# Newton step and scale factor of a group norm moved from VectorE to GpSimd in a convolution kernel

## The chip, the cores and the metric

The kernel runs on one core of a Trainium2 chip. The metric is the device time of one launch, in microseconds (us). The engines are called by the profile's names: PE is TensorE (matrix products), DVE is VectorE, ACT is ScalarE, POOL is GpSimd, SP is SyncE, which here only issues transfers.

## What is computed

Input x holds 32 images of 128 channels with 56 rows of 56 columns, float32. Each image is normalised in 32 groups of 4 channels, convolved with 3x3 weights that are first made ternary, and added to x.

```python
def _gn(v, G=32, eps=1e-05):
    B_, C_, H_, W_ = v.shape
    g = v.reshape(B_, G, C_ // G, H_, W_)
    m = jnp.mean(g, axis=(2, 3, 4), keepdims=True)
    s = jnp.var(g, axis=(2, 3, 4), keepdims=True)
    return ((g - m) / jnp.sqrt(s + eps)).reshape(v.shape)
...
wq = _quantize(weight, Wp, Wn)
out = jax.lax.conv_general_dilated(x, wq, window_strides=(1, 1), padding=((1, 1), (1, 1)), ...)
return out + bias[None, :, None, None]
...
x = x + _L0_conv_ref(_gn(x), L0_conv_weight, L0_conv_bias, L0_conv_Wp, L0_conv_Wn)
```

## The kernel before, in words

The 128 channels lie on the 128 partitions; one image is 128 x 3136 float32. The program handles one image in a slot, and the engines work on neighbouring images at once: in the slot of image `now` PE multiplies `now`, while DVE and ACT prepare image `nxt`, and ACT takes the sums of image `far`. Each engine's order inside a slot is written out by hand in a function `emit`; engines wait for each other by semaphores alone. The loop body holds four slots, since x and y have four buffers each.

For the rows of the convolution, even and odd image rows are combined into four planes C, D, A, B of 128 x 1568 float32 (sums and differences of rows): `make_c` (L561), `make_d` (L567) and `make_a` (L573) on DVE, `difference_b` (L326) on POOL. Each plane is multiplied by the image's scale factor `norm_scale` (one number for each partition) and split in two float16 parts: HI on ACT (`make_hi`, L388) and LO, the scaled plane minus HI, on DVE (`make_lo`, L607). PE multiplies the parts by the weights, 24 matmuls for each plane (L766). ACT copies the products of C and D out of the accumulators (L373, L379), and DVE adds the products of A and B to them in four instructions (`output_rows`, L622). POOL then issues two transfers that add x to y (L339), and SP stores y.

The scale factor of `nxt` is made in a chain of small steps on 128 x 1 numbers. PE sums the squares (L757), DVE makes the negative variance (`variance`, L585), ACT takes the root (`root`, L440), DVE takes the reciprocal (`first_rstd`, L591), and DVE refines it by one Newton step in two instructions (`newton_factor`, L596, and `scale_of_x`, L602). ACT's `make_hi(nxt, C)` is the first instruction that reads the result, and it waits for the semaphore `scale_of_x_ready`. DVE reads it first in `make_lo(nxt, C)`, behind that HI.

In a slot of the loop DVE's order is: LO of D, variance of `nxt`, LO of A, planes C and D of `nxt`, the three small steps, LO of B, plane A of `nxt`, LO of C of `nxt`, four output instructions. "LO of D, A, B" are those of `now`. POOL's order is plane B of `nxt`, then the two transfers of `now`. Plane B waits for LO of B and LO of C on DVE (`lo_ready`), and it thus stands beside DVE's output instructions. There are 30 slots of this kind; the first two slots have orders of their own.

Of the kernel before, what the change touches and what calls it, by code (L numbers as in the profile page):

```python
# [6 lines left out]
P = 128  # L7
# [4 lines left out]
X_BUFS = 4  # L12
# [10 lines left out]
ALU = mybir.AluOpType  # L23
# [7 lines left out]
def conv_preact_kernel(nc, x, weight, bias, wp, wn, out):  # L31
# [15 lines left out]
    with ExitStack() as ctx:  # L47
        def sb(name, shape, dt=F32):
            return ctx.enter_context(nc.sbuf_tensor(name, shape, dt))

        def sem(name):
            return ctx.enter_context(nc.semaphore(name))
# [33 lines left out]
        neg_var = sb("neg_var", [P, X_BUFS])  # L86
        std = sb("std", [P, X_BUFS])
        rstd0 = sb("rstd0", [P, X_BUFS])
        newton = sb("newton", [P, X_BUFS])
        norm_scale = sb("norm_scale", [P, X_BUFS])  # L90


# [39 lines left out]
        var_ready = sem("var_ready")  # L132
        std_ready = sem("std_ready")
        rstd_ready = sem("rstd_ready")
        newton_ready = sem("newton_ready")
        scale_of_x_ready = sem("scale_of_x_ready")
        edges_ready = sem("edges_ready")
        plane_ready = [sem(f"plane_ready{j}") for j in range(4)]
# [61 lines left out]
        def b_slice(img):  # L200
            return slice(img.buf, img.buf + 1)
# [98 lines left out]
        def _(pool):  # L300
# [17 lines left out]
                                        pattern=[[-1, P]], channel_multiplier=1).then_inc(consts_ready, 1)  # L318

            def run(p):  # L320
                def difference_b(img):
                    pool.wait_ge(x_loaded[img.buf], img.turn * 32 + 32)
                    wait(pool, lo_ready[B], img.count())
                    pool.wait_ge(lo_ready[C], img.count(plus=1))
                    even = x_sb[img.buf][:, 0:H:2, :]
                    nc.gpsimd.tensor_tensor(plane[B][:, 0:PAIRS - 1, :], even[:, 0:PAIRS - 1, :], even[:, 1:, :],  # L326
                                            ALU.subtract).then_inc(plane_ready[B], 1)

                def add_residual(img, h):

                    written = img.half(h, 1, 1)
                    if not isinstance(written, int):
                        written = pool.to_reg(written)
                    pool.wait_ge(consts_ready, 2 + len(TURNS))
                    pool.wait_ge(even_done, written)
                    pool.wait_ge(odd_done, written)
                    y = y_sb[img.buf][:, 2 * ROWS * h:2 * ROWS * (h + 1), :].rearrange("p h w -> p (h w)")
                    of = (out_dram if p else x_dram)[img.count(plus=-p * N_IMG)][:, h * 2 * COLS:(h + 1) * 2 * COLS]
                    pool.dma_start(y, of, accum_op=ALU.add).then_inc(residual_added[img.buf][h], 16)  # L339

                def emit(prev, now, nxt, far):
                    if now and nxt:
                        difference_b(nxt)
                    if now and nxt:
                        add_residual(now, 0)
                        add_residual(now, 1)

                slots(p, pool, emit)

            run(0)  # L350
            pool.wait_ge(flag_ready, 1)
            with pool.If(pool.value_load(differ[0:1, 0:1], min_val=0, max_val=1) != 0):
# [142 lines left out]

        @block.vector
        def _(dve):
            nc.vector.memset(no_bias[:], 0.0).then_inc(zero_ready, 1)

            steps = [0]  # L500
# [44 lines left out]
            def run(p):  # L545
# [44 lines left out]
                    dve.wait_ge(std_ready, img.count(plus=1))  # L590
                    nc.vector.reciprocal(rstd0[:, b], std[:, b]).then_inc(rstd_ready, 1)  # L591

                def newton_factor(img):
                    b = b_slice(img)
                    dve.wait_ge(rstd_ready, img.count(plus=1))
                    nc.vector.tensor_scalar(newton[:, b], rstd0[:, b], rstd0[:, b], neg_var[:, b],  # L596
                                            ALU.mult, ALU.mult).then_inc(newton_ready, 1)

                def scale_of_x(img):
                    b = b_slice(img)  # L600
                    dve.wait_ge(newton_ready, img.count(plus=1))
                    nc.vector.tensor_scalar(norm_scale[:, b], newton[:, b], 3.0, rstd0[:, b],  # L602
                                            ALU.add, ALU.mult).then_inc(scale_of_x_ready, 1)

                def make_lo(img, j):
                    dve.wait_ge(hi_ready[j], img.count(plus=1))
                    nc.vector.scalar_tensor_tensor(part(img, j, LO), plane[j][:], norm_scale[:, b_slice(img)],  # L607
# [39 lines left out]
                def emit(prev, now, nxt, far):  # L647
                    first_slot, second_slot = not now and not prev, now and not prev
                    if first_slot:
                        if p == 0:  # L650
                            local_max()
                        make_d(nxt)
                        if p == 0:
                            ternary_weights()
                        variance(nxt)
                        make_c(nxt)
                        first_rstd(nxt)
                        newton_factor(nxt)
                        scale_of_x(nxt)
                        turned_weights((C, D))  # L660
                        make_first_lo(nxt)
                    if second_slot:
# [7 lines left out]
                        make_lo(now, A)  # L670
                        make_c(nxt)
                        first_rstd(nxt)
                        newton_factor(nxt)
                        scale_of_x(nxt)
                        make_lo(now, B)
                        make_d(nxt)
                        make_lo(nxt, C)
                    elif now:
# [6 lines left out]
                        make_lo(now, A)  # L685
                        if nxt:
                            make_c(nxt)
                            make_d(nxt)
                            first_rstd(nxt)
                            newton_factor(nxt)  # L690
                            scale_of_x(nxt)
                        make_lo(now, B)
                        if nxt:
                            make_a(nxt)
# [171 lines left out]
```

## Time and profile before

| | us |
|---|---|
| median of 3 runs (lowest, highest) | 567.59 (567.28, 568.82) |
| the profiled execution's own time | 566.68 |
| its span, first to last instruction | 565.0 |
| DVE busy | 543.4 (96%) |
| PE busy | 531.7 (94%) |
| ACT busy | 504.1 (89%) |
| POOL busy | 162.6 (29%) |

The span is what the trace covers; 1.7 us of the profiled execution lie outside it. "Busy" is the time in which an engine has an instruction in flight. Neighbouring instructions of one engine overlap by some 0.08 us, so a start-to-start distance tells what an instruction costs its engine better than its duration does.

### The profile page before, as it was taken

The page shows a single profiled execution, that of the slowest core. Times are in us where ns is not written, and L with a number is a line of the kernel's source. Part 1 is how long each engine was busy: PE and PEld are TensorE (multiplying, and loading weights), DVE is VectorE, ACT ScalarE, POOL GpSimd, SP SyncE. Part 2 cuts the span into 40 slices and gives each one's busy share as a digit, 9 for nine tenths or more (in the row PEclk, how much of TensorE's full clock was granted, in tenths as well). Part 3 has the DMA queues.
Part 4 walks back from the last instruction along what each step waited for, and adds up shares of the span by engine and source line. Part 5 has one row for each costly group of instructions (what it writes and reads, how often), then busy time and mean ns, then how long its engine had stood idle before and what let it go on. Part 6 is the DMA issues. An engine that isn't in the chain of part 4 may idle for free.

```text
span 565.0 us, 9357 instructions
## 1 busy us (share of the span) xinstructions
PE 531.7 (94%) x3233; PEld 319.3 (57%) x3233; DVE 543.4 (96%) x506; ACT 504.1 (89%) x485; POOL 162.6 (29%) x106
## 2 busy tenths in 40 slices
PE   1898999999999999999999999999999999999994
PEld 0654555655555555555555555556555555555552
DVE  4998999999999999999999999999999999999994
ACT  4898999999999999999999999999999999999850
POOL 2030333311333331233332123333113333312330
PEclk9999999999999999999999999999999999999998
DMA  8439799999999999999999999999999999998767
GB/s 295 202 115 256 239 286 293 293 261 266 289 299 288 313 278 270 294 294 318 297 297 278 279 298 261 309 282 302 268 301 277 292 289 304 293 281 195 155 180 276
DMA packets 28105, 153.43 MB, mean 272 GB/s; under 512 B 3505, under 2 KB 3505, under 8 KB 28081
## 3 DMA queue, kind: packets, MB, share of 16 engines
q1 hardware_dynamic: 18576, 102.77, 48.2%
q0 software_dynamic: 8928, 49.78, 45.5%
q10 hardware_dynamic: 576, 0.59, 0.3%
q8 instruction: 12, 0.20, 0.1%
q14 instruction: 13, 0.10, 0.0%
HBM read 101.75 MB, written 51.38 MB: 271 GB/s over the span
## 4 chain that ended last, share of the span: by engine, by line
DVE 69%; issue 23%; PE 2%; ACT 2%; DMA 1%; DVEq 1%; ACTq 0%
DVE parts L607 26%; DVE y L622 19%; DVE plane L561 10%; DVE plane L567 9%; DVE newton L596 2%; PE odd_rows L766 1%; DMA x<-in_x_dram 1%; DVE plane L573 1%; PE even_rows L766 1%; DVEq L157 1%; DVE neg_var L585 1%; ACT junk L434 1%; DVE rstd L591 0%; DVE parts L613 0%; ACT junk L394 0%
## 5 line engine op out<-in xcount | busy, mean ns | idle before, releaser
L766 PE MATMUL odd_rows<-parts,w_lhsT 128*128 128x385 f16 (+1 forms) x1536 | 266.1, 330 | 7.8 <-DVE parts L607 7.5
L766 PE MATMUL even_rows<-parts,w_lhsT 128*128 128x385 f16 (+1 forms) x1536 | 265.6, 330 | 3.6 <-ACT c_sb L373 2.3
L607 DVE SCALAR_TENSOR_TENSOR parts<-plane,norm_scale,parts 128x1568 f16<-128x1568 f32 x127 | 233.5, 1843 | 1.7 <-ACT parts L388 1.7
L326 POOL TENSOR_TENSOR plane<-x 128x1512 f32<-128x1512 f32 x31 | 105.8, 3412 | 379.1 <-DVE parts L607 379.1
L766 PEld LDWEIGHTS even_rows<-parts,w_lhsT 128*128 128x128 f16 x1536 | 149.3, 98 | 110.0 <-issue 4.9
L388 ACT ACTIVATE parts<-plane,norm_scale 128x1568 f16<-128x1568 f32 x127 | 199.9, 1597 | 11.8 <-ACT plane L428 5.2
L766 PEld LDWEIGHTS odd_rows<-parts,w_lhsT 128*128 128x128 f16 x1536 | 147.9, 99 | 107.3 <-DVE parts L607 9.8
L434 ACT ACTIVATE junk<-x,negmean 128x3136 f16<-128x3136 f32 x32 | 92.9, 2904 | 0.1
L394 ACT ACTIVATE junk<-x 128x3136 f16<-128x3136 f32 x31 | 86.9, 2804 | 0.0
L622 DVE SCALAR_TENSOR_TENSOR y<-even_rows,out_scale,d_sb 128x784 f32<-128x784 f32 x62 | 61.0, 1026 | 0.0
L622 DVE SCALAR_TENSOR_TENSOR y<-odd_rows,out_scale,c_sb 128x784 f32<-128x784 f32 x62 | 60.9, 1024 | 0.0
L561 DVE SCALAR_TENSOR_TENSOR plane<-x,neg2mean 128x1568 f32<-128x1568 f32 x32 | 59.0, 1845 | 0.0
L567 DVE TENSOR_TENSOR plane<-x 128x1568 f32<-128x1568 f32 x32 | 57.1, 1784 | 0.4 <-ACT junk L402 0.4
L379 ACT ACTIVATE d_sb<-odd_rows,bias_sb,out_scale 128x1568 f32<-128x1568 f32 x32 | 52.6, 1643 | 5.3 <-PE odd_rows L766 5.3
L573 DVE TENSOR_TENSOR plane<-x 128x1512 f32<-128x1512 f32 x32 | 55.2, 1725 | 0.0
L339 POOL DMA_DIRECT2D y<-in_x_dram x62 | 54.3, 887 | 3.2 <-DVE y L622 0.5
L373 ACT ACTIVATE c_sb<-even_rows,bias_sb,out_scale 128x1568 f32<-128x1568 f32 x32 | 52.5, 1641 | 0.5 <-DVE out_scale L543 0.4
L419 ACT ACTIVATE neg2mean<-odd_rows 128x1 f32<-128x1 f32 x32 | 5.4, 170 | 22.7 <-PE odd_rows L752 21.6
L757 PEld LDWEIGHTS odd_rows<-sums,group_mean 128*128 128x128 f32 x64 | 11.6, 194 | 5.6 <-issue 3.5
L752 PEld LDWEIGHTS odd_rows<-sums,group_mean 128*128 128x128 f32 x62 | 11.2, 195 | 3.4 <-DVE parts L607 0.9
L757 PE MATMUL odd_rows<-sums,group_mean 128*128 128x1 f32 x64 | 9.2, 213 | 3.4 <-ACT junk L434 3.4
L427 ACT ACTIVATE plane<-x,negmean 128x56 f32<-128x56 f32 x32 | 10.6, 332 | 0.0
(65 smaller groups left out, 109.9 us busy)
## 6 DMA issues: line engine op xcount, KB each, us to landing
x<-in_x_dram SPq DMA_DIRECT2D x64, 784.0 KB, 11.0
out_dram<-y SPq DMA_DIRECT2D x63, 784.0 KB, 5.6
y<-in_x_dram POOLq DMA_DIRECT2D x62, 784.0 KB, 11.9
out_dram<-y SPq DMA_DIRECT2D x2, 392.0 KB, 5.9
y<-in_L_conv_weight_dram ACTq DMA_DIRECT2D x1, 576.0 KB, 6.7
wp_sb<-in_L_conv_Wp_dram ACTq DMA_DIRECT2D x1, 0.5 KB, 7.7
wn_sb<-in_L_conv_Wn_dram ACTq DMA_DIRECT2D x1, 0.5 KB, 7.9
bias_sb<-in_L_conv_bias_dram ACTq DMA_DIRECT2D x1, 0.5 KB, 7.6
```

Of the source, the lines that this page charges most:

```text
L326: nc.gpsimd.tensor_tensor(plane[B][:, 0:PAIRS - 1, :], even[:, 0:PAIRS - 1, :], even[:, 1:, :], ALU.subtract).then_inc(plane_ready[B], 1)
L339: pool.dma_start(y, of, accum_op=ALU.add).then_inc(residual_added[img.buf][h], 16)
L379: nc.scalar.activation(d_sb[:], product_ps(ODD), ACT.Identity, bias=(no_bias if p else bias_sb)[:, 0:1], scale=out_scale[:, p, 1:2]).then_ ...
L388: nc.scalar.activation(part(img, j, HI), plane[j][:], ACT.Copy, scale=norm_scale[:, b_slice(img)]).then_inc(hi_ready[j], 1)
L394: nc.scalar.activation(junk[:], x_sb[img.buf][:].rearrange("p h w -> p (h w)"), ACT.Copy, accum_out=sums[:, img.buf, 1:2]).then_inc(sum_re ...
L434: nc.scalar.activation(junk[:], x_sb[img.buf][:].rearrange("p h w -> p (h w)"), ACT.Square, bias=negmean[:, b_slice(img)], accum_out=sums[ ...
L561: nc.vector.scalar_tensor_tensor(plane[C][:], xs[:, 0:H:2, :], neg2mean[:, b_slice(img)], xs[:, 1:H:2, :], ALU.add, ALU.add).then_inc(plan ...
L567: nc.vector.tensor_tensor(plane[D][:], xs[:, 1:H:2, :], xs[:, 0:H:2, :], ALU.subtract).then_inc(plane_ready[D], 1)
L573: nc.vector.tensor_tensor(plane[A][:, 1:, :], odd[:, 1:, :], odd[:, 0:PAIRS - 1, :], ALU.subtract).then_inc(plane_ready[A], 1)
L607: nc.vector.scalar_tensor_tensor(part(img, j, LO), plane[j][:], norm_scale[:, b_slice(img)], part(img, j, HI), ALU.mult, ALU.subtract).the ...
L622: nc.vector.scalar_tensor_tensor(rows_of(y_sb[img.buf], h, odd), product_ps(odd, 2 * h, 2 * h + 2), out_scale[:, p, 0:1], other[:, 2 * h:2 ...
L766: ins = nc.tensor.matmul(product_ps(odd, b, b + 1)[:, 0, :, to:to + n], w_lhsT[:, prod, kw, :], part(img, prod, which)[:, b * BANK_ROWS:(b ...
```

## The change

The two DVE instructions of the Newton step are taken away. POOL computes the same in four products and sums on 128 x 1 numbers: the square of the first reciprocal, times the negative variance, plus three, times the first reciprocal. Each of the four waits for the one before it, by a new semaphore `newton_step`. They stand at the start of POOL's slot, ahead of plane B and of the two transfers. In a slot of the loop the reciprocal stays on DVE but moves from behind plane D to between planes C and D. A constant tile of threes is set once at the start, and POOL waits for it once.

```diff
             def run(p):
+                def scale_of_x(img):
+
+                    b = b_slice(img)
+                    pool.wait_ge(rstd_ready, img.count(plus=1))
+                    nc.gpsimd.tensor_tensor(rstd_sq[:, b], rstd0[:, b], rstd0[:, b], ALU.mult).then_inc(newton_step, 1)
+                    pool.wait_ge(newton_step, img.count(3, 1))
+                    nc.gpsimd.tensor_tensor(less[:, b], rstd_sq[:, b], neg_var[:, b], ALU.mult).then_inc(newton_step, 1)
+                    pool.wait_ge(newton_step, img.count(3, 2))
+                    nc.gpsimd.tensor_tensor(newton[:, b], less[:, b], three[:], ALU.add).then_inc(newton_step, 1)
+                    pool.wait_ge(newton_step, img.count(3, 3))
+                    nc.gpsimd.tensor_tensor(norm_scale[:, b], newton[:, b], rstd0[:, b],
+                                            ALU.mult).then_inc(scale_of_x_ready, 1)
+
...
                 def emit(prev, now, nxt, far):
+                    if nxt:
+                        scale_of_x(nxt)
                     if now and nxt:
                         difference_b(nxt)
...
+            pool.wait_ge(zero_ready, 1)
             run(0)
...
         def _(dve):
+            nc.vector.memset(three[:], 3.0)
             nc.vector.memset(no_bias[:], 0.0).then_inc(zero_ready, 1)
...
-                def newton_factor(img):
-                    b = b_slice(img)
-                    dve.wait_ge(rstd_ready, img.count(plus=1))
-                    nc.vector.tensor_scalar(newton[:, b], rstd0[:, b], rstd0[:, b], neg_var[:, b],
-                                            ALU.mult, ALU.mult).then_inc(newton_ready, 1)
-
-                def scale_of_x(img):
-                    b = b_slice(img)
-                    dve.wait_ge(newton_ready, img.count(plus=1))
-                    nc.vector.tensor_scalar(norm_scale[:, b], newton[:, b], 3.0, rstd0[:, b],
-                                            ALU.add, ALU.mult).then_inc(scale_of_x_ready, 1)
-
...
                         make_c(nxt)
                         first_rstd(nxt)
-                        newton_factor(nxt)
-                        scale_of_x(nxt)
                         make_lo(now, B)
                         make_d(nxt)
                         make_lo(nxt, C)
...
                         if nxt:
                             make_c(nxt)
+                            first_rstd(nxt)
                             make_d(nxt)
-                            first_rstd(nxt)
-                            newton_factor(nxt)
-                            scale_of_x(nxt)
                         make_lo(now, B)
```

In the first slot the two instructions behind the reciprocal go away in the same manner.

DVE's program in a slot of the loop, from LO of D to the first output instructions, before the change. L607 is a LO, L585 the variance, L561, L567 and L573 are planes C, D and A, L591 to L602 the three small steps, L622 the outputs:

```order
L607 SCALAR_TENSOR_TENSOR parts<-plane,norm_scale,parts 128x1568
L585 TENSOR_SCALAR neg_var<-odd_rows 128x1
L607 SCALAR_TENSOR_TENSOR parts<-plane,norm_scale,parts 128x1568
L561 SCALAR_TENSOR_TENSOR plane<-x,neg2mean 128x1568
L567 TENSOR_TENSOR plane<-x 128x1568
L591 RECIPROCAL rstd<-std 128x1
L596 TENSOR_SCALAR newton<-rstd,neg_var 128x1
L602 TENSOR_SCALAR norm_scale<-newton,rstd 128x1
L607 SCALAR_TENSOR_TENSOR parts<-plane,norm_scale,parts 128x1568
L573 TENSOR_TENSOR plane<-x 128x1512
L607 SCALAR_TENSOR_TENSOR parts<-plane,norm_scale,parts 128x1568
L622 SCALAR_TENSOR_TENSOR y<-even_rows,out_scale,d_sb 128x14x56 x2
```

The same place after the change; the line numbers are those of the changed program, where L615 is a LO, L605 the variance, L581, L587 and L593 are planes C, D and A, L611 is the reciprocal, L630 an output:

```order
L615 SCALAR_TENSOR_TENSOR parts<-plane,norm_scale,parts 128x1568
L605 TENSOR_SCALAR neg_var<-odd_rows 128x1
L615 SCALAR_TENSOR_TENSOR parts<-plane,norm_scale,parts 128x1568
L581 SCALAR_TENSOR_TENSOR plane<-x,neg2mean 128x1568
L611 RECIPROCAL rstd<-std 128x1
L587 TENSOR_TENSOR plane<-x 128x1568
L615 SCALAR_TENSOR_TENSOR parts<-plane,norm_scale,parts 128x1568
L593 TENSOR_TENSOR plane<-x 128x1512
L615 SCALAR_TENSOR_TENSOR parts<-plane,norm_scale,parts 128x1568
L630 SCALAR_TENSOR_TENSOR y<-even_rows,out_scale,d_sb 128x14x56 x2
```

Two small instructions are gone, and the reciprocal stands one plane earlier: between it and LO of C of `nxt` DVE now has plane D, LO of B and plane A.

POOL's program in one slot before the change is plane B and the two transfers:

```order
L324 REGISTER_ALU
L326 TENSOR_TENSOR plane<-x 128x1512
L333 REGISTER_ALU
L339 ISA
L339 DMA y<-in_x_dram 128x1568
```

After the change the four small instructions stand ahead of plane B (L342), with a register computation for the count that each waits for:

```order
L327 REGISTER_ALU
L328 TENSOR_TENSOR rstd_sq<-rstd 128x1
L329 REGISTER_ALU
L330 TENSOR_TENSOR less<-rstd_sq,neg_var 128x1
L331 REGISTER_ALU
L332 TENSOR_TENSOR newton<-less,three 128x1
L333 REGISTER_ALU
L334 TENSOR_TENSOR norm_scale<-newton,rstd 128x1
L342 TENSOR_TENSOR plane<-x 128x1512
```

POOL has four instructions and three waits on itself between DVE's reciprocal and the signal that ACT's HI of C waits for.

## Rows read from the trace of the kernel before

**Rows 1.** The page: busy time by engine; the chain that ended last, by engine.

```profile
PE 531.7 (94%) x3233; PEld 319.3 (57%) x3233; DVE 543.4 (96%) x506; ACT 504.1 (89%) x485; POOL 162.6 (29%) x106
...
DVE 69%; issue 23%; PE 2%; ACT 2%; DMA 1%; DVEq 1%; ACTq 0%
```

**Rows 2.** Stages: start:end, length, busy of PE, PEld, DVE, ACT, POOL, clock, DMA share, GB/s.

```profile
40.00:60.00 20.00, 17.22 (x105) 9.82 (x103) 18.28 (x17) 18.02 (x17) 5.25 (x4) 1.00 0.83 242
...
244.36:260.97 16.61, 16.36 (x102) 9.86 (x100) 16.54 (x16) 15.64 (x16) 5.14 (x4) 1.00 1.02 295
```

**Rows 3.** Waits from 200 to 500 us: total us, times, longest.

```profile
ACT neg2mean L419 <- PE odd_rows L752: 13.9, 18, 0.8
...
PE odd_rows L766 <- DVE parts L607: 4.4, 18, 0.2
...
PEld even_rows L766 <- DVE y L622: 2.6, 17, 0.2
```

**Rows 4.** DVE in order of time, one slot: start us, us, instruction.

```profile
244.36 1.84 DVE L607 SCALAR_TENSOR_TENSOR parts<-plane,norm_scale,parts 128x1568 f16<-128x1568 f32 x1
...
246.19 1.84 DVE L607 SCALAR_TENSOR_TENSOR parts<-plane,norm_scale,parts 128x1568 f16<-128x1568 f32 x1
...
247.94 1.84 DVE L561 SCALAR_TENSOR_TENSOR plane<-x,neg2mean 128x1568 f32<-128x1568 f32 x1
249.71 1.78 DVE L567 TENSOR_TENSOR plane<-x 128x1568 f32<-128x1568 f32 x1
251.41 0.15 DVE L591 RECIPROCAL rstd<-std 128x1 f32<-128x1 f32 x1
251.60 0.27 DVE L596 TENSOR_SCALAR newton<-rstd,neg_var 128x1 f32<-128x1 f32 x1
251.91 0.21 DVE L602 TENSOR_SCALAR norm_scale<-newton,rstd 128x1 f32<-128x1 f32 x1
252.04 1.84 DVE L607 SCALAR_TENSOR_TENSOR parts<-plane,norm_scale,parts 128x1568 f16<-128x1568 f32 x1
253.80 1.72 DVE L573 TENSOR_TENSOR plane<-x 128x1512 f32<-128x1512 f32 x1
255.44 1.84 DVE L607 SCALAR_TENSOR_TENSOR parts<-plane,norm_scale,parts 128x1568 f16<-128x1568 f32 x1
...
260.97 1.84 DVE L607 SCALAR_TENSOR_TENSOR parts<-plane,norm_scale,parts 128x1568 f16<-128x1568 f32 x1
```

**Rows 5.** ACT and POOL in order of time in the same slot.

```profile
252.16 1.60 ACT L388 ACTIVATE parts<-plane,norm_scale 128x1568 f16<-128x1568 f32 x1
...
254.55 0.17 ACT L419 ACTIVATE neg2mean<-odd_rows 128x1 f32<-128x1 f32 x1 [0.80 <-PE odd_rows L752]
...
257.37 3.40 POOL L326 TENSOR_TENSOR plane<-x 128x1512 f32<-128x1512 f32 x1 [11.35 <-DVE parts L607]
```

**Rows 6.** Groups by shape: busy us, mean ns, idle before; POOL's and DVE's outputs.

```profile
L326 POOL TENSOR_TENSOR plane<-x 128x1512 f32<-128x1512 f32 x31 | 105.8, 3412 | 379.1 <-DVE parts L607 379.1
...
L310 POOL TENSOR_SCALAR_AFFINE_SELECT ident<-ident 128x128 f32<-128x128 f32 x1 | 0.3, 292 | 0.0
...
L855 POOL MEMSET const-bfloat16-1.0<- 128x1 bf16 x1 | 0.1, 101 | 0.0
...
L622 DVE SCALAR_TENSOR_TENSOR y<-odd_rows,out_scale,c_sb 128x784 f32<-128x784 f32 x62 | 60.9, 1024 | 0.0
...
L644 DVE SCALAR_TENSOR_TENSOR y<-even_rows,out_scale,d_sb 128x784 f32<-128x784 f32 x2 | 2.0, 1030 | 0.1
```

**Rows 7.** Order of time: POOL at the start; POOL and ACT in the last slot.

```profile
1.22 0.42 POOL L303 MEMSET turn<- 128x384 f16 x1
...
1.71 0.52 POOL L308 TENSOR_SCALAR_AFFINE_SELECT group_mean<-group_mean 128x128 f32<-128x128 f32 x1
...
539.96 3.41 POOL L326 TENSOR_TENSOR plane<-x 128x1512 f32<-128x1512 f32 x1 [11.52 <-DVE parts L607]
...
543.45 1.60 ACT L388 ACTIVATE parts<-plane,norm_scale 128x1568 f16<-128x1568 f32 x1 [3.47 <-POOL plane L326]
```

More of the change, by code:

```diff
@@ L88, in conv_preact_kernel @@
         rstd0 = sb("rstd0", [P, X_BUFS])
+        rstd_sq = sb("rstd_sq", [P, X_BUFS])
+        less = sb("less", [P, X_BUFS])
         newton = sb("newton", [P, X_BUFS])
+        three = sb("three", [P, 1])
         norm_scale = sb("norm_scale", [P, X_BUFS])
@@ L134, in conv_preact_kernel @@
         rstd_ready = sem("rstd_ready")
-        newton_ready = sem("newton_ready")
+        newton_step = sem("newton_step")
         scale_of_x_ready = sem("scale_of_x_ready")
@@ L687, in emit @@
                             make_c(nxt)
+                            first_rstd(nxt)
                             make_d(nxt)
-                            first_rstd(nxt)
-                            newton_factor(nxt)
-                            scale_of_x(nxt)
                         make_lo(now, B)
```

## The prediction

> **What bounds the kernel now.** I read the page first. DVE is busy for 96% of the span and PE for 94%, and 69% of the chain that ended last is DVE's [rows 1]. Two engines that close can't be told apart by shares, so I took one slot of the loop, from one LO of plane D to the next [rows 4]: 244.36 to 260.97, or 16.61 us. In that stretch DVE is busy for 16.54 us, PE for 16.36, ACT for 15.64 [rows 2]. Then the waits of 18 slots: DVE doesn't appear among those who wait. PE waits for DVE twice in a slot, 4.4 / 18 = 0.24 us for LO of D and 2.6 / 17 = 0.15 us for the first output, and ACT waits once, 0.80 us, for PE's sum of the mean [rows 3, 5]. So DVE's own row of instructions sets the 16.61 us, PE could do with 16.61 - 0.24 - 0.15 = 16.22 us, and ACT with about 15.8. Whatever shortens DVE's row is worth at most 0.39 us in a slot before PE is the bound, and whatever makes DVE wait is paid in full, in each of 30 slots and in much the same form in the second slot: 31 times.
>
> **What is taken from DVE.** From the start of plane D to the start of LO of B pass 252.04 - 249.71 = 2.33 us [rows 4]. Plane D alone would take 251.41 - 249.71 = 1.70, so the three small steps cost 0.63 us: each waits for the one before. The reciprocal remains. Between two planes nothing behind it waits for it. The variance stands like that between two LOs: with it they start 246.19 - 244.36 = 1.83 us apart, and a LO without it costs 253.80 - 252.04 = 1.76 [rows 4], so such a step costs 0.07. DVE's row gets 0.63 - 0.07 = 0.56 us shorter.
>
> **What POOL's chain costs by itself.** The trace has no 128x1 product on POOL. From below: its 128x1 memset takes 0.10 us; from above: the select over 128 columns takes 0.29; plane B takes 3.41 for 1512 columns, or 2.26 ns a column at most, which leaves little beside a fixed part [rows 6]. I take 0.15 us, nearer to the memset, since there is one column. Between an instruction and the POOL instruction that waits for it pass 1.71 - 1.64 = 0.07 us (the memset from 1.22 lasts 0.42). From POOL's end to ACT's start pass 543.45 - 543.37 = 0.08 [rows 7], from DVE's LO of C (ended at 257.28) to POOL's start 0.09 [rows 4, 5]. The chain undisturbed is 0.09 + 4 x 0.15 + 3 x 0.07 + 0.08 = 0.98 us. The reciprocal would end at 249.71 + 0.15 = 249.86, the chain at 250.84, and ACT begins HI of C, the first reader, at 252.16 [rows 5]. 1.3 us would be left: even at 0.29 us for each product the chain would be hidden behind ACT's copy of D's product. In the queue behind the four stand plane B, which starts at 257.37, and the two transfers. None is held up. If this were all, the change would gain.
>
> **What it meets.** Where will POOL read its numbers? DVE's plane D starts just after the reciprocal, then come LO of B and plane A without a gap [rows 4]. All of these read two operands of full length from the on-chip memory (two halves of x, or a plane and its HI). The only instruction with which POOL reads there before is plane B, and it always stands elsewhere: from 257.37 to 260.77, beside the outputs, which read one operand from the accumulators and one from memory; LO of D follows at 260.97 [rows 4, 5]. An output beside POOL takes 1.02 us, without it 1.03 [rows 6]: one operand is no hindrance. Of the two-operand case there is no instance in 31 slots, so the trace clears POOL only for the places where it doesn't go any more. I therefore price the case in which a POOL read and a two-operand DVE instruction exclude each other.
>
> The Trainium skill, page "SBUF — State Buffer", section "Who interferes with whom", states just that: a VectorE instruction with two SBUF inputs contends with a GpSimd instruction that reads SBUF, and whichever comes second waits for the whole of the first. By this rule the sum is the one below, and by the undisturbed chain above it is that of the first rival; no run here shows yet which holds.
>
> Plane D is in flight when the reciprocal's signal reaches POOL. Two orders are possible behind it. *POOL comes last*: DVE's instructions follow each other so closely that POOL gets in only when DVE stops, and DVE stops at LO of C, which waits for HI of C, which waits for POOL. From the end of plane A it then takes 0.09 to start, 4 x 0.15 + 3 x 0.07 + 0.08 = 0.89, HI of C 1.60 [rows 5], and 0.08 to DVE: 2.66 us, and 0.08 more since LO of C now starts that much ahead of plane A's end (255.44 against 255.52) [rows 4]. That is 2.74 us of standstill. *They take turns*: the square goes in behind plane D, the second product behind LO of B, the sum behind plane A, the last at once. The standstill is 0.08 + 0.09 + 2 x 0.15 + 0.07 + 0.08 + 1.60 + 0.08 = 2.30, and two breaks in DVE's row cost 0.15 + 0.08 each: 2.76 together. Both orders cost the same, so I needn't choose.
>
> What is late next? ACT's HI of C starts 1.68 us before LO of C where it was 3.28; the 0.80 us wait at L419 takes up half of that, and the other half finds room, since HI of A ends well before its LO and ACT needs only 15.8 us of the longer slot. PE waits about 2.5 us a slot for LO of C or D. Its clock should hold: from 40 to 60 us it was busy for 17.22 of 20.00 at a granted clock of 1.00 [rows 2], and 16.36 of 18.8 is as much.
>
> **The sum.** 2.75 - 0.56 = +2.2 us a slot, 31 times: +68 us. The first slot adds nothing: the copies on DVE there read the accumulators, and ACT is busy with the next image's sum. 566.68, the profiled execution's own time, + 68 = 634.7; the median lies 0.9 above it, so 635. With products of 0.10 us in the first order it is 2.0 a slot, 629; with 0.29 us 2.75, 653.
>
> **The rivals.**
> 1. *No hindrance*: the products run beside plane D. DVE's row is 16.05, PE then binds at 16.22, the gain is 31 x 0.39 = 12 us: 555 (550 if PE's stalls shrink as well and all 0.56 counts). For it: one column for each partition is next to nothing to read, 1.3 us of slack, DVE surely rid of 0.56 us. Against it: all four reads fall under two-operand instructions, for which no row vouches. Ends on the other side; it decides as soon as the chain ends by about 252.2. Chance 0.13.
> 2. *A turn for all*: POOL gets in behind plane D and keeps LO of B out until its four are done. DVE loses 0.98 and gains 0.56: +0.4 us a slot, 579. For it: the waits between the four are only 0.07 long. Against it: LO of B stands ready without any wait. Chance 0.05.
> 3. *No change*: something else holds the slot at 16.61. The transfers have a share of 1.02 at 295 GB/s [rows 2], which could be their limit. Against it: no compute engine waits for a transfer in 18 slots, and ACT's and PE's waits are all for engines. Chance 0.05.
>
> **How the numbers follow.** The forecast case has 0.77: that an engine pair so close needs no exclusion is possible, but the change puts every product into the one combination that the trace leaves open, and both orders within it end at the same price. A measurement of this kernel tells a difference from about 0.3%, or 1.7 us. Slower: 0.77 + 0.05 = 0.82; same: 0.05; faster: 0.13. The likeliest case alone spans 620 to 655: 629 with the shortest product and some 9 us for a stall that ACT's lateness or the order shortens, 653 with the longest. With rival 2 the range is 576 to 655, and some 2 in 10 are left out.
>
> **What would show it.** Right: the first product on POOL starts not 0.1 but 1.7 us or more behind the reciprocal; either the four stand together behind plane A, or one behind each of D, B and A; DVE idles some 2.3 to 2.7 us before LO of C, put down to ACT's HI; ACT idles before HI of C with POOL as releaser; a slot lasts near 18.8 us; plane B on POOL still takes 3.41. Wrong: products at 249.95 or so with plane D above them, a slot near 16.2, and PE without waits. Wrong in size: products longer than 0.29 us, gaps of POOL's queue for its registers between them, or planes on DVE that last longer than 1.78 because they share and don't exclude.

## The result and the profile after

The changed kernel takes 625.33 us (624.17 to 626.60, 4 runs) against 567.43 us before: ratio 1.102, 95% interval 1.100 to 1.104. It is slower by 57.9 us; 635 was forecast, with 576 to 655 as the range. The span of the profiled execution grew from 565.0 to 622.3 us, by 57.3.

The page of the changed kernel: busy time by engine and the chain that ended last, as in [rows 1]:

```profile
PE 537.9 (86%) x3233; PEld 316.1 (51%) x3233; DVE 530.5 (85%) x443; ACT 503.6 (81%) x485; POOL 328.0 (53%) x234
...
POOL 40%; issue 25%; DVE 18%; ACT 10%; PE 3%; POOLq 2%; DMA 1%; DVEq 0%; ACTq 0%
```

DVE lost 13 us of work, as it should, and is now idle for 15% of the span. POOL, which was given four instructions of one column for each image, is busy for 165 us more, and the chain runs through it. The waits from 200 to 500 us, as in [rows 3] (total us, times, longest):

```profile
ACT parts L407 <- POOL norm_scale L334: 41.3, 16, 2.6
DVE parts L615 <- ACT parts L407: 36.0, 16, 2.3
...
PE even_rows L768 <- DVE y L630: 24.6, 16, 1.5
```

Read from the top this is the new stall with what is behind it, in each slot: ACT's HI of C waits 2.6 us for the scale factor, DVE's LO of C 2.25 us for that HI, PE 1.5 us for the outputs behind that LO. One slot in order of time, the counterpart of [rows 4, 5]; L581, L587, L593 are planes C, D, A, L611 the reciprocal, L615 a LO, L407 a HI, L328 to L334 POOL's four products:

```profile
250.64 1.85 DVE L615 SCALAR_TENSOR_TENSOR parts<-plane,norm_scale,parts 128x1568 f16<-128x1568 f32 x1
...
254.22 1.85 DVE L581 SCALAR_TENSOR_TENSOR plane<-x,neg2mean 128x1568 f32<-128x1568 f32 x1
255.98 0.16 DVE L611 RECIPROCAL rstd<-std 128x1 f32<-128x1 f32 x1
256.06 1.78 DVE L587 TENSOR_TENSOR plane<-x 128x1568 f32<-128x1568 f32 x1
256.23 1.66 POOL L328 TENSOR_TENSOR rstd_sq<-rstd 128x1 f32<-128x1 f32 x1 [3.93 <-DVE rstd L611]
...
257.75 1.85 DVE L615 SCALAR_TENSOR_TENSOR parts<-plane,norm_scale,parts 128x1568 f16<-128x1568 f32 x1
257.96 3.32 POOL L330 TENSOR_TENSOR less<-rstd_sq,neg_var 128x1 f32<-128x1 f32 x1
259.51 1.73 DVE L593 TENSOR_TENSOR plane<-x 128x1512 f32<-128x1512 f32 x1
...
261.37 0.19 POOL L332 TENSOR_TENSOR newton<-less,three 128x1 f32<-128x1 f32 x1
261.63 0.19 POOL L334 TENSOR_TENSOR norm_scale<-newton,rstd 128x1 f32<-128x1 f32 x1
261.86 1.60 ACT L407 ACTIVATE parts<-plane,norm_scale 128x1568 f16<-128x1568 f32 x1 [2.56 <-POOL norm_scale L334]
...
263.49 1.85 DVE L615 SCALAR_TENSOR_TENSOR parts<-plane,norm_scale,parts 128x1568 f16<-128x1568 f32 x1 [2.25 <-ACT parts L407]
...
265.26 1.97 DVE L630 SCALAR_TENSOR_TENSOR y<-even_rows,out_scale,d_sb 128x784 f32<-128x784 f32 x2
265.49 3.41 POOL L342 TENSOR_TENSOR plane<-x 128x1512 f32<-128x1512 f32 x1 [3.67 <-DVE parts L615]
...
269.03 1.84 DVE L615 SCALAR_TENSOR_TENSOR parts<-plane,norm_scale,parts 128x1568 f16<-128x1568 f32 x1
```

Look at ends, not starts (an end is start plus duration). The first product ends at 256.23 + 1.66 = 257.89, 0.05 us behind the end of plane D (257.84). The second ends at 261.28, 0.04 behind the end of plane A (261.24), and LO of B ended in between without letting it go. The last two, with DVE standing still, take 0.19 us each. One and the same kind of instruction on 128 x 1 numbers thus takes 0.19, 1.66 or 3.32 us, and which of these it is depends on what DVE does. It is the same in the 30 slots of the loop: 1.65 or 1.66, 3.32 or 3.33, 0.19, 0.19. The slot, from LO of D to LO of D, is 269.03 - 250.64 = 18.39 us long, where it was 16.61.

The ledger of a slot, in distances from start to start: from plane D to LO of B pass 257.75 - 256.06 = 1.69 us instead of 2.33; the reciprocal costs 0.07 between C and D, whose starts are 256.06 - 254.22 = 1.84 us apart and were 1.77; from plane A to LO of C pass 263.49 - 259.51 = 3.98 us instead of 1.64. So -0.64 + 0.07 + 2.34 = +1.77, and 31 times that is 55 us; the remaining 2 us lie in the first slots and behind the last image.

### The profile page after: what moved, and what is told of

Its sections match the earlier page's. It is cut to its first block, busy times and chain, and to the rows that moved or that the text cites. A ratio compares the mean times of both kernels' runs of the same rounds, so it can differ in the third digit from the quotient of the medians.

```text
span 622.3 us, 9501 instructions
## 1 busy us (share of the span) xinstructions
PE 537.9 (86%) x3233; PEld 316.1 (51%) x3233; DVE 530.5 (85%) x443; ACT 503.6 (81%) x485; POOL 328.0 (53%) x234
## 4 chain that ended last, share of the span: by engine, by line
POOL 40%; issue 25%; DVE 18%; ACT 10%; PE 3%; POOLq 2%; DMA 1%; DVEq 0%; ACTq 0%
POOL less L330 16%; DVE parts L615 11%; POOL plane L342 10%; POOL rstd_sq L328 9%; ACT parts L407 8%; DVE y L630 4%; POOL y L355 4%; PE odd_rows L768 2%; DVE plane L581 1%; DMA x<-in_x_dram 1%; POOL newton L332 1%; POOL norm_scale L334 1%; ACT junk L413 1%; PE even_rows L768 1%; DVE plane L593 1%
## 5 line engine op out<-in xcount | busy, mean ns | idle before, releaser
L615 DVE SCALAR_TENSOR_TENSOR parts<-plane,norm_scale,parts 128x1568 f16<-128x1568 f32 x127 | 233.9, 1847 | 71.4 <-ACT parts L407 71.4
L407 ACT ACTIVATE parts<-plane,norm_scale 128x1568 f16<-128x1568 f32 x127 | 200.0, 1598 | 90.7 <-POOL norm_scale L334 80.8
L768 PEld LDWEIGHTS odd_rows<-parts,w_lhsT 128*128 128x128 f16 x1536 | 146.0, 99 | 111.7 <-DVE parts L615 11.0
L342 POOL TENSOR_TENSOR plane<-x 128x1512 f32<-128x1512 f32 x31 | 105.7, 3411 | 114.2 <-DVE parts L615 114.2
L328 POOL TENSOR_TENSOR rstd_sq<-rstd 128x1 f32<-128x1 f32 x32 | 53.3, 1665 | 149.0 <-DVE rstd L611 149.0
L330 POOL TENSOR_TENSOR less<-rstd_sq,neg_var 128x1 f32<-128x1 f32 x32 | 100.1, 3129 | 2.5
L630 DVE SCALAR_TENSOR_TENSOR y<-odd_rows,out_scale,c_sb 128x784 f32<-128x784 f32 x62 | 61.1, 1027 | 1.0 <-PE odd_rows L768 1.0
L630 DVE SCALAR_TENSOR_TENSOR y<-even_rows,out_scale,d_sb 128x784 f32<-128x784 f32 x62 | 61.1, 1027 | 0.0
L581 DVE SCALAR_TENSOR_TENSOR plane<-x,neg2mean 128x1568 f32<-128x1568 f32 x32 | 59.1, 1848 | 0.0
L587 DVE TENSOR_TENSOR plane<-x 128x1568 f32<-128x1568 f32 x32 | 56.8, 1776 | 0.6 <-ACT junk L421 0.6
L593 DVE TENSOR_TENSOR plane<-x 128x1512 f32<-128x1512 f32 x32 | 55.4, 1731 | 0.0
```

What stands on the lines that cost most here:

```text
L328: nc.gpsimd.tensor_tensor(rstd_sq[:, b], rstd0[:, b], rstd0[:, b], ALU.mult).then_inc(newton_step, 1)
L330: nc.gpsimd.tensor_tensor(less[:, b], rstd_sq[:, b], neg_var[:, b], ALU.mult).then_inc(newton_step, 1)
L407: nc.scalar.activation(part(img, j, HI), plane[j][:], ACT.Copy, scale=norm_scale[:, b_slice(img)]).then_inc(hi_ready[j], 1)
L581: nc.vector.scalar_tensor_tensor(plane[C][:], xs[:, 0:H:2, :], neg2mean[:, b_slice(img)], xs[:, 1:H:2, :], ALU.add, ALU.add).then_inc(plan ...
L593: nc.vector.tensor_tensor(plane[A][:, 1:, :], odd[:, 1:, :], odd[:, 0:PAIRS - 1, :], ALU.subtract).then_inc(plane_ready[A], 1)
L630: nc.vector.scalar_tensor_tensor(rows_of(y_sb[img.buf], h, odd), product_ps(odd, 2 * h, 2 * h + 2), out_scale[:, p, 0:1], other[:, 2 * h:2 ...
```

## The experiments

The theory: a POOL instruction that reads the on-chip memory and a DVE instruction that reads two operands from it exclude each other, so that one can't run while the other does. Its rivals: POOL's chain is slow or late by itself (issue, registers of the loop, semaphores), or the reciprocal's new place does the harm. L-numbers shift by some lines from kernel to kernel.

**Only the reciprocal moved** (Newton step left on DVE):

```diff
                             make_c(nxt)
+                            first_rstd(nxt)
                             make_d(nxt)
-                            first_rstd(nxt)
                             newton_factor(nxt)
                             scale_of_x(nxt)
```

> Newton step stays on DVE behind plane D; only the reciprocal moves, to between planes C and D. Both theories (exclusion of POOL's reads and DVE's two-operand instructions; POOL merely slow) expect the same here, since POOL does nothing new: DVE's row loses the reciprocal's wait, 0.63 to about 0.51 us a slot, so 0.12 x 30 = 3.7 us, ratio about 0.994. If the move itself were what hurts in the changed kernel, this would be slower than before.

563.71 us (563.23 to 564.59), ratio 0.993 [0.991, 0.994]: as expected, and the fastest of all kernels here that compute the reference. The move is innocent, and by itself worth 3.8 us.

**The four products beside it, with nobody waiting for them** (the kernel of the last run, with the products put on POOL as well):

```diff
+                def spare_products(img):
+                    b = b_slice(img)
+                    pool.wait_ge(rstd_ready, img.count(plus=1))
+                    nc.gpsimd.tensor_tensor(spare[0][:, b], rstd0[:, b], rstd0[:, b], ALU.mult).then_inc(spare_step, 1)
...
                     dve.wait_ge(var_summed, img.count(plus=1))
+                    wait(dve, spare_done, img.count(plus=1 - X_BUFS))
```

> As e1, and POOL computes the same four products beside it into tiles that nobody reads (only the next use of the same buffer, four images on, waits for them). Exclusion with POOL as the loser: first product about 1.66 us, second about 3.3, last two 0.19 as in the changed kernel, and DVE unhurt, so the time is that of e1, about 564 us. Exclusion with turns that cost DVE too: plane D to LO of B longer by up to 0.2 us, so up to 570. POOL merely slow in the loop: products longer whatever DVE does, time as e1.

566.0 us (565.02 to 568.45), ratio 0.998 [0.996, 0.999]. One slot of it; L586 is plane D, L592 plane A, L616 and L622 the Newton step on DVE, L627 a LO:

```profile
250.23 1.78 DVE L586 TENSOR_TENSOR plane<-x 128x1568 f32<-128x1568 f32 x1
250.40 1.66 POOL L328 TENSOR_TENSOR spare<-rstd 128x1 f32<-128x1 f32 x1 [3.93 <-DVE rstd L611]
...
252.13 0.19 POOL L330 TENSOR_TENSOR spare<-spare,neg_var 128x1 f32<-128x1 f32 x1
...
252.36 1.84 DVE L627 SCALAR_TENSOR_TENSOR parts<-plane,norm_scale,parts 128x1568 f16<-128x1568 f32 x1
252.40 1.85 POOL L332 TENSOR_TENSOR spare<-spare,three 128x1 f32<-128x1 f32 x1
...
254.11 1.73 DVE L592 TENSOR_TENSOR plane<-x 128x1512 f32<-128x1512 f32 x1
254.33 1.56 POOL L334 TENSOR_TENSOR spare<-spare,rstd 128x1 f32<-128x1 f32 x1
```

Three of POOL's four products are long here too, each ending 0.05 us behind a DVE instruction of full length; only the one that meets DVE's small steps is short. DVE's own distances are those of the kernel without the products (250.23 to 251.91, where the small steps begin, 1.68 against 1.69; plane A to LO of C 1.65 in both). So the harm isn't that DVE is slowed by the small products but that somebody waits for them. I had expected 1.66 and 3.3 for the first two; the small steps of DVE gave POOL a gap that I had overlooked. Of the 2.3 us above the kernel without products the distances above explain nothing. In every second slot the variance starts 0.1 us later behind its LO than without the products (1.92 us against 1.82), which is 1.4 us in all. PE's sum is no later there, it ends 1.79 us behind the start of that LO in both; but the variance starts 0.13 us behind the sum and not 0.04. This run has a second wait ahead of the variance, for `spare_done`. That this wait costs the 0.1 us, and not the products, is likely but wasn't tested.

**Plane D from one operand**, in the changed kernel; the even rows aren't subtracted:

```diff
+                def make_d_of_one(img):
+                    plane_free(img, D)
+                    odd = x_sb[img.buf][:, 1:H:2, :].rearrange("p h (w o) -> p h w o", o=1)
+                    nc.vector.tensor_reduce(plane[D][:], odd, AX_X, ALU.max).then_inc(plane_ready[D], 1)
...
                             first_rstd(nxt)
-                            make_d(nxt)
+                            make_d_of_one(nxt)
```

> The changed kernel, but in the loop plane D is made by a reduction over one element, which reads one operand (odd rows only; the subtraction of the even rows is left out), with about the same length. Exclusion: all four products run during it at 0.19 us each, the factor is ready ahead of ACT's HI of C, and the slot falls from 18.4 to about 16.2 us, where PE binds: 553 to 558 us. POOL merely slow, or late by its queue: products stay at 1.66 and 3.3 us and the time stays at 625.

561.76 us (561.28 to 562.15), ratio 0.990 [0.988, 0.992]. From the same kind of view; L593 is now plane D:

```profile
249.94 0.16 DVE L616 RECIPROCAL rstd<-std 128x1 f32<-128x1 f32 x1
250.01 1.77 DVE L593 TENSOR_REDUCE plane<-x 128x1568 f32<-128x1568 f32 x1
...
250.18 0.19 POOL L328 TENSOR_TENSOR rstd_sq<-rstd 128x1 f32<-128x1 f32 x1 [4.26 <-DVE rstd L616]
250.44 0.19 POOL L330 TENSOR_TENSOR less<-rstd_sq,neg_var 128x1 f32<-128x1 f32 x1
250.71 0.19 POOL L332 TENSOR_TENSOR newton<-less,three 128x1 f32<-128x1 f32 x1
...
250.98 0.19 POOL L334 TENSOR_TENSOR norm_scale<-newton,rstd 128x1 f32<-128x1 f32 x1
...
252.44 1.60 ACT L407 ACTIVATE parts<-plane,norm_scale 128x1568 f16<-128x1568 f32 x1
```

This decides it. DVE's instruction stands at the same place and lasts as long (1.77 us), writes as much, and reads one operand less; all four products run under it, 0.27 us from start to start, and are done at 251.17. The loss of 58 us is gone. The chain is neither slow nor late by itself. The instruction differs in its operation as well, a reduction instead of a subtraction, but the operation can't be what matters: DVE's outputs are of the same operation as its LOs, with one operand from the accumulators, and plane B on POOL takes its usual 3.41 us beside them in the changed kernel too (265.49 to 268.90). That the gain stops at 0.990 is mostly PE's doing: from 200 to 500 us it is busy for 100.00 of each 100 us, and slots alternate between 16.22 and 16.37 or 16.38, mean 16.30. And some 3 us more than in the kernel before are spent in the first slots, which the edit leaves alone: in the second one the first product takes 3.43 us and DVE stands still for 2.53 us before LO of C.

**The small steps on DVE, one in each gap** (kernel before):

```diff
+                            first_rstd(nxt)
                             make_c(nxt)
+                            newton_factor(nxt)
                             make_d(nxt)
-                            first_rstd(nxt)
-                            newton_factor(nxt)
                             scale_of_x(nxt)
```

> All on DVE, POOL as before: reciprocal ahead of plane C, Newton factor between C and D, scale factor behind D, so that each small step has a long instruction between itself and the one it waits for. Each costs DVE about 0.07 to 0.1 us instead of 0.63 for the three: 0.33 to 0.39 us a slot, 30 slots, 10 to 12 us faster (555 to 558, ratio about 0.98), with PE as the next bound. Against it: the reciprocal waits for ACT's root, which ends at 247.91 where it would start at 247.95; if ACT falls behind, DVE waits ahead of plane C and the gain shrinks.

566.01 us (565.51 to 566.57), ratio 0.997 [0.996, 0.998]: a miss. Slots alternate between 16.36 and 16.76 us, mean 16.56, where 16.22 to 16.28 was hoped for. In the short ones the three steps cost 0.37 us together, 0.08, 0.17 and 0.12, and not 0.07 to 0.1 each. In the long ones the variance starts 1.96 us behind its LO instead of 1.76, just behind the end of PE's sum, and the reciprocal 1.84 to 1.90 us behind its LO instead of 1.76, just behind the end of the root (one slot: root to 265.43, reciprocal from 265.46). In the kernel before the variance doesn't wait and the reciprocal stands 3.5 us behind the root. The earlier place costs nearly all that the gaps give.

**The reciprocal earlier still** (changed kernel, ahead of plane C):

```diff
                         if nxt:
+                            first_rstd(nxt)
                             make_c(nxt)
-                            first_rstd(nxt)
                             make_d(nxt)
```

> The changed kernel with the reciprocal one instruction earlier still, ahead of plane C, so that POOL's chain could start 1.8 us sooner. Exclusion: nothing gained, because the wait ends with plane A as before; the first product is in flight from plane C to the end of plane D (about 3.4 us), the second again to the end of plane A, time 625 us or a few more for the reciprocal's wait for the root. If POOL's chain were just late by its own latency: 1.8 us a slot back, the standstill of 2.25 us nearly gone, time near 570.

632.85 us (632.65 to 633.05), ratio 1.114 [1.105, 1.122]. If the chain were just late, its head start of one instruction, 1.8 us, would come back nearly whole. It doesn't: the kernel is slower still, so lateness by itself isn't the cause. The products' groups in its profile (mean ns of one in front of the idle time):

```profile
L328 POOL TENSOR_TENSOR rstd_sq<-rstd 128x1 f32<-128x1 f32 x32 | 55.8, 1744 | 119.7 <-DVE rstd L611 119.7
...
L332 POOL TENSOR_TENSOR newton<-less,three 128x1 f32<-128x1 f32 x32 | 50.9, 1589 | 2.5
L330 POOL TENSOR_TENSOR less<-rstd_sq,neg_var 128x1 f32<-128x1 f32 x32 | 49.0, 1531 | 2.5
```

Here each product costs one DVE instruction: in all slots of the loop but one they end 0.04 to 0.06 us behind planes C, D, LO of B and plane A. I had expected the first to be carried over two; wrong. The head start buys no more than this: all four are done at the end of plane A instead of two behind it, so that from plane A to LO of C pass 3.45 us instead of 3.98. Against that DVE waits 0.68 us for the root ahead of the reciprocal, and the slot is 18.64 to 18.76 us long.

The one other slot is 17.15 us long. In it the first product isn't held by plane C, and the chain ends one DVE instruction earlier:

```profile
110.02 1.88 DVE L581 SCALAR_TENSOR_TENSOR plane<-x,neg2mean 128x1568 f32<-128x1568 f32 x1
110.07 0.19 POOL L328 TENSOR_TENSOR rstd_sq<-rstd 128x1 f32<-128x1 f32 x1 [2.71 <-DVE rstd L611]
```

It starts 0.05 us behind the start of plane C. In 11 other slots it starts 0.05 to 0.07 us behind it, and takes 1.84 or 1.85 us.

**Plane A ahead of LO of B** (changed kernel):

```diff
+                            make_a(nxt)
                         make_lo(now, B)
                         if nxt:
-                            make_a(nxt)
                             make_lo(nxt, C)
```

> The changed kernel with planes D, A and then LO of B on DVE (before: D, LO of B, A). Two readings of why POOL's second product is carried over two DVE instructions where the first is released after one: (a) POOL gets in ahead of a LO, which has a scale factor to fetch first, and not ahead of a plane: then the first product lasts to the end of plane A (about 3.3 us) and the second to the end of LO of B (about 1.85); (b) whatever product comes second is carried over two: first 1.66, second about 3.5. The time by either is that of the changed kernel, 625 us, plus up to 1 us a slot if PE misses LO of B.

624.25 us (623.62 to 624.88), ratio 1.099 [1.090, 1.107]: the same slot, 18.39 us. Now the first product is carried over two and the second is not:

```profile
255.41 1.77 DVE L587 TENSOR_TENSOR plane<-x 128x1568 f32<-128x1568 f32 x1
255.58 3.30 POOL L328 TENSOR_TENSOR rstd_sq<-rstd 128x1 f32<-128x1 f32 x1 [3.93 <-DVE rstd L611]
...
258.75 1.84 DVE L615 SCALAR_TENSOR_TENSOR parts<-plane,norm_scale,parts 128x1568 f16<-128x1568 f32 x1
258.96 1.68 POOL L330 TENSOR_TENSOR less<-rstd_sq,neg_var 128x1 f32<-128x1 f32 x1
```

So it isn't the second product's nature. Reading (a), that POOL gets in ahead of a LO and not ahead of a plane, fits this run and the changed kernel, but its second half doesn't fit the one with the earlier reciprocal, where it got in ahead of plane D and of plane A. Its first half holds throughout: in all profiles here, those below too, a POOL instruction that waits under a plane with a LO next gets in before that LO, 242 times of 242. Ahead of a plane it gets in in some slots and not in others. Why isn't shown.

**Two products on POOL instead of four** (DVE keeps the first Newton instruction, between planes C and D):

```diff
-                    pool.wait_ge(rstd_ready, img.count(plus=1))
-                    nc.gpsimd.tensor_tensor(rstd_sq[:, b], rstd0[:, b], rstd0[:, b], ALU.mult).then_inc(newton_step, 1)
-                    pool.wait_ge(newton_step, img.count(3, 1))
-                    nc.gpsimd.tensor_tensor(less[:, b], rstd_sq[:, b], neg_var[:, b], ALU.mult).then_inc(newton_step, 1)
...
                     nc.vector.reciprocal(rstd0[:, b], std[:, b]).then_inc(rstd_ready, 1)
+                    dve.wait_ge(rstd_ready, img.count(plus=1))
+                    nc.vector.tensor_scalar(less[:, b], rstd0[:, b], rstd0[:, b], neg_var[:, b],
+                                            ALU.mult, ALU.mult).then_inc(less_ready, 1)
```

> Half of the change: DVE keeps the first Newton instruction, right behind the reciprocal between planes C and D; POOL only adds three and multiplies. DVE's row is longer by about 0.3 us. Exclusion that carries the second product to the end of plane A as in the changed kernel: the standstill loses only the two free products, 0.53 us, a slot of about 18.2 us, 618 us. If instead each product costs one DVE instruction, the second is released behind LO of B, ACT's HI of C starts about 1.9 us late instead of 3.4, a slot near 17, about 585. If the number of products is what costs, half of the loss is gone: 596.

593.33 us (591.83 to 594.83), ratio 1.044 [1.034, 1.054]. That is close to "half the products, half the loss", and yet not for that reason: the slots are of two kinds, 16.55 us and 18.18 us, in no order that I can see; the last product is the long one in 14 slots of 30. I had expected 18.2 or 17 us, one of them throughout. Two of them, in order of time, L331 being the last product; the first is of the short kind, the second of the long one:

```profile
189.46 1.66 POOL L329 TENSOR_TENSOR newton<-less,three 128x1 f32<-128x1 f32 x1 [4.21 <-DVE less L610]
191.20 1.68 POOL L331 TENSOR_TENSOR norm_scale<-newton,rstd 128x1 f32<-128x1 f32 x1
...
242.37 1.66 POOL L329 TENSOR_TENSOR newton<-less,three 128x1 f32<-128x1 f32 x1 [4.24 <-DVE less L610]
...
244.11 3.33 POOL L331 TENSOR_TENSOR norm_scale<-newton,rstd 128x1 f32<-128x1 f32 x1
```

In the loop the last product always starts 0.21 or 0.22 us behind the start of LO of B, and is released either at that LO's end or only at plane A's. It looks like a race for the gap between two DVE instructions.

**A memset of one column in that gap**, in the kernel with two products and in the changed one:

```diff
                         make_lo(now, B)
                         if nxt:
+                            nc.vector.memset(gap[:], 0.0)
                             make_a(nxt)
```

> The kernel with two products on POOL, and a memset of one column on DVE between LO of B and plane A. In the profile without it the second product was released behind LO of B in some slots (16.55 us each) and carried on to the end of plane A in others (18.2 us), with the same start in both. If it is a close race for the gap between two DVE instructions, the small instruction widens the gap and all slots go the short way: 16.6 us a slot, 565 to 568 us. If something else decides, slots stay mixed and the time stays near 593.

> The changed kernel with the same memset between LO of B and plane A. If the gap is what POOL lacked: first product to the end of plane D, second to the end of LO of B, third (instead of second) to the end of plane A, only the last one free: 0.27 us less standstill, 0.07 more row, so 0.2 us a slot, 619 us. If the gap doesn't matter, 1.66 and 3.33 as before and 627.

With two products: 567.12 us (566.30 to 568.95), ratio 1.000 [0.998, 1.001], 26 us faster than without the memset. The slots behind the second are all 16.53 to 16.59 us. With four: 616.47 us (616.16 to 616.77), ratio 1.086 [1.083, 1.090], 8.9 us faster than the changed kernel, and its slots behind the second are all 18.13 or 18.14. There the second product now goes behind LO of B (L616) and the third takes its place under plane A (L594):

```profile
255.26 1.84 DVE L616 SCALAR_TENSOR_TENSOR parts<-plane,norm_scale,parts 128x1568 f16<-128x1568 f32 x1
255.47 1.68 POOL L331 TENSOR_TENSOR less<-rstd_sq,neg_var 128x1 f32<-128x1 f32 x1
257.04 1.73 DVE L594 TENSOR_TENSOR plane<-x 128x1512 f32<-128x1512 f32 x1
257.06 0.06 DVE L697 MEMSET gap<- 128x1 f32 x1
257.24 1.57 POOL L333 TENSOR_TENSOR newton<-less,three 128x1 f32<-128x1 f32 x1
258.89 0.19 POOL L335 TENSOR_TENSOR norm_scale<-newton,rstd 128x1 f32<-128x1 f32 x1
```

One column written on DVE decides whether POOL gets in: with the memset it does in 30 slots of 30, in both kernels. How it does so isn't shown. I had expected the memset to widen the gap, but plane A starts 1.76 to 1.78 us behind LO of B with it and 1.76 or 1.77 without it, and the memset, which stands ahead of plane A in the program, is recorded 0.02 us behind plane A's start. A race that some hundredths of a microsecond decide fits these numbers; so does a rule by which an instruction without operands, standing between the two, lets POOL in. What decides without the memset stays open too.

**The other way round: POOL has the memory and DVE comes second** (kernel before; plane B on POOL no longer waits for LO of C):

```diff
                     wait(pool, lo_ready[B], img.count())
-                    pool.wait_ge(lo_ready[C], img.count(plus=1))
```

> The kernel before, but POOL's plane B (3.4 us, reads two operands) no longer waits for LO of C of the next image and so becomes ready as soon as LO of B is done, while DVE runs plane A and then LO of C. It asks what exclusion costs when POOL is the one that has the memory: DVE should stand still for up to 3.4 us behind plane A or LO of B, a slot of up to 20 us, 600 to 670 us; plane B by itself would last longer than 3.41 where it comes second. Without exclusion: nothing changes but POOL's time, 567 us.

709.94 us (709.43 to 710.46), ratio 1.251 [1.247, 1.255]. L572 is plane A, L606 LO of C, L325 plane B:

```profile
249.52 1.73 DVE L572 TENSOR_TENSOR plane<-x 128x1512 f32<-128x1512 f32 x1
249.69 4.82 POOL L325 TENSOR_TENSOR plane<-x 128x1512 f32<-128x1512 f32 x1 [10.61 <-DVE parts L606]
...
251.16 5.00 DVE L606 SCALAR_TENSOR_TENSOR parts<-plane,norm_scale,parts 128x1568 f16<-128x1568 f32 x1
```

By its ends, plane B waits for plane A's (251.25) and then needs 3.26 us, about its usual 3.41, to 254.51; LO of C, begun at 251.16, takes 5.00 instead of 1.84 us and ends 1.65 us behind plane B. It is so for all 31 images, 4.98 to 5.01 us. Whoever comes second waits for the whole of the first, in both directions. The Trainium skill, page "SBUF — State Buffer", section "Who interferes with whom", states this; the trace agrees, with these numbers. Who is second can't be read from the starts in the profile, though: the second product of the changed kernel starts 1.55 us ahead of plane A (257.96 against 259.51) and is still the one that waits. LO of C's delay alone is 3.16 x 31 = 98 us of the 142. For the rest see, of the same kernel, first the waits from 200 to 500 us, then two stages (start:end, length, busy of PE, PEld, DVE, ACT, POOL, clock, DMA share, GB/s):

```profile
DVE neg_var L584 <- PE odd_rows L756: 22.6, 13, 2.6
```

```profile
254.00:260.00 6.00, 2.96 (x11) 1.35 (x11) 6.00 (x6) 4.32 (x6) 0.81 (x2) 0.80 0.58 186
257.17:263.01 5.84, 5.84 (x27) 3.11 (x28) 4.52 (x4) 1.32 (x1) 1.74 (x2) 0.71 0.89 288
```

PE waits 3.04 us for the first output behind the long LO and so is idle for half of these 6 us; its granted clock, 1.00 from 248 to 254 (that is 2.4 GHz), is 0.80 in them. The 24 matmuls that begin at 257.17 take 5.84 us, where 24 of the same size take 4.15 at 249.97; the clock over them is 0.71, between its levels of 1.2 and 2.4 GHz, and 4.15 / 5.84 is 0.71 too. The 1.69 us that they take longer are about what DVE then waits for PE's sum, 22.6 / 14 = 1.6 us a slot (from 200 to 500 us there are 14), or 50 us in all. The two together come to 148 us, near enough to 142, though I didn't test the clock's part by itself.

## Why the prediction was right, point by point

- **DVE bounds the slot, 0.56 us are taken from it.** Right: 0.57.
- **The chain would be hidden if undisturbed.** Right: with plane D from one operand it is done 1.27 us ahead of ACT's HI of C (252.44 against 251.17). Each product takes 0.19 us where I took 0.15, and 0.27 from one to the next where I had 0.22.
- **POOL's reads and DVE's two-operand instructions exclude each other.** Right, shown by that run and in the other direction by plane B.
- **Two orders at one price.** The mechanism was right, and this term is the one that was mis-sized: 2.75 us of standstill and breaks, measured 2.34. Neither order occurred. The first product went behind plane D as in "they take turns", the second missed the gap behind LO of B as in "POOL comes last", so two products stood behind plane A, which is where "they take turns" leaves two as well. Its standstill was put at 2.30 us, and 2.34 is measured. What was wrong are the 0.46 us for two breaks in DVE's row: they cost DVE nothing. A waiting product fits into the hand-over from one DVE instruction to the next, and D to LO of B takes 1.69 us with it and 1.70 without [rows 4]. So the orders don't cost the same, and I should have chosen; it was some luck that the one that occurred, which I hadn't listed, lies only 0.4 us a slot or 13 us below the forecast, of which 2 to 3 us came back at the ends.
- **PE would hold its clock.** Right for the changed kernel, 1.00 in the loop at 16.55 us of work in 18.40. PE's waits are shorter than the 2.5 us that I put them at, and mostly elsewhere: 1.5 us for the first output and 0.3 for a LO. It wasn't so behind a wait of 3 us (plane B at once).
- **Rival 1, 555 us.** Its price was 0.39 us a slot with PE at 16.22; with the exclusion lifted from plane D PE binds at 16.30, and the time is 561.8, of which 3 us are the first slots'.
- **Rival 2, a turn for all.** In no profile here does POOL keep DVE out until a chain of small products is done: between two dependent products DVE's next instruction takes its place.
- **Rival 3, something else holds the slot.** No: the slot went up to 18.39 us here and down to 16.30 with plane D from one operand, there at the same DMA share of 1.02 as before.

## What to carry to other kernels

What an instruction costs on POOL can't be read from its size: look at what DVE runs at that moment and how many operands that reads from the on-chip memory. Work that nobody waits for may go to POOL at little cost (2 us at most here), but a chain of dependent small steps can pay one or two long DVE instructions for each step; if it must be there, put it beside DVE instructions with one operand, or give it gaps. Look at the ends: when short instructions of one engine end just behind long ones of another, they share something.

## What I had not expected

A 128 x 1 memset of 0.06 us between two DVE instructions makes a kernel 26 us faster (593.3 to 567.1), because with it POOL always gets in ahead of plane A, where without it it does so in 16 slots of 30. Before that, one and the same program had slots of 16.55 and 18.18 us side by side, which a mean over the span would hide.
